# Routing the first two images as two groups of one in a conv-attention and mixture-of-experts kernel

## What is computed

```
x = x + conv_ref(ln_c(x))            # rmsnorm, qkv, softmax of q over dims, of k over pixels,
                                     # context = k v^T, out = context q, W_out, rmsnorm
t = to_tokens(x)                     # (16, 1024, 128)
logits = ln_t(t) @ gate_w + gate_b   # 8 experts
top2 of softmax(logits)
t = t + sum over both experts e of  p_e * (gelu(ln_t(t) @ W1[e] + b1[e]) @ W2[e] + b2[e])
```

## Time and profile before

| what | value |
|---|---|
| median of 3 runs | 974.99 us (972.36 to 977.9) |
| profiled execution | 973.93 us |
| its span, first to last instruction | 972.1 us |
| mean granted TensorE clock | 0.872 of full |
| PE busy | 699.5 us (72%) |
| POOL busy | 596.0 us (61%) |
| DVE busy | 589.4 us (61%) |
| ACT busy | 505.0 us (52%) |
| mean DMA rate | 178 GB/s |

### The profile page before, as it was taken

The page is one execution under the profiler, slowest core; times in us unless marked ns, Lnnn a source line. Parts: engine busy times, 40 slices in busy tenths (PEclk is TensorE's granted clock), DMA queues, the critical chain, the costliest instruction groups (busy, mean ns, idle before and its releaser), DMA issues. The chain is left out here.

```text
span 972.1 us, 15703 instructions
## 1 busy us (share of the span) xinstructions
PE 699.5 (72%) x4357; PEld 598.2 (62%) x4357; DVE 589.4 (61%) x1913; ACT 505.0 (52%) x980; POOL 596.0 (61%) x602
## 2 busy tenths in 40 slices
PE   4645738696979596969696878778796886778700
PEld 2433626686868485858585867666675775667600
DVE  2587484849475958495848676776768555233322
ACT  2423223675757566657656666756765544335400
POOL 1013636534457577757777677757775777777374
PEclk9867666897979898979998998989997998989955
DMA  6301012656656675766676776766566776779622
GB/s 165 104 22 36 30 57 75 212 171 199 188 185 199 191 224 165 228 206 192 205 221 190 226 219 198 207 211 207 170 212 201 221 238 205 254 234 309 221 77 63
DMA packets 120574, 173.46 MB, mean 178 GB/s; under 512 B 20504, under 2 KB 82600, under 8 KB 120488
## 3 DMA queue, kind: packets, MB, share of 16 engines
q1 hardware_dynamic: 103352, 138.65, 46.6%
q0 software_dynamic: 16384, 33.59, 11.5%
q10 hardware_dynamic: 752, 0.21, 0.1%
HBM read 112.86 MB, written 62.14 MB: 180 GB/s over the span
## 5 line engine op out<-in xcount | busy, mean ns | idle before, releaser
L465 POOL DMA_INDIRECT rows_in<-xf_tok,row_of x256 | 257.2, 1005 | 100.0 <-issue 77.6
L479 POOL DMA_INDIRECT y_rows<-rows_out,row_back x256 | 250.2, 977 | 93.3 <-issue 69.7
L1005 PE MATMUL y_ps<-wb,hid 128*128 128x128 f32 x1472 | 212.7, 291 | 65.8 <-DVE yb L869 56.0
L1005 PEld LDWEIGHTS y_ps<-wb,hid 128*128 128x128 f32 x1472 | 201.9, 205 | 90.1 <-issue 60.4
L559 ACT ACTIVATE hid<-h_ps,wb 128x256 f32<-128x256 f32 x368 | 158.4, 473 | 106.5 <-PE h_ps L995 104.8
L995 PE MATMUL h_ps<-xt,wb 128*128 128x256 f32 x736 | 204.3, 403 | 0.0
L869 DVE TENSOR_TENSOR yb<-y_ps,wb 128x256 f32<-128x256 f32 x184 | 77.4, 421 | 159.4 <-PE y_ps L1005 158.9
L995 PEld LDWEIGHTS h_ps<-xt,wb 128*128 128x128 f32 x736 | 137.3, 205 | 19.2
L553 ACT ACTIVATE xt<-t_ps 128x256 f32<-128x256 f32 x184 | 70.7, 384 | 131.2 <-PE t_ps L986 130.3
L919 PE MATMUL ab<-wqkv_t,x_sb 128*128 128x384 f32 x256 | 109.8, 524 | 10.2 <-ACT qkv L517 10.0
L517 ACT ACTIVATE qkv<-ab,r 128x384 f32<-128x384 f32 x128 | 73.3, 582 | 61.5 <-PE ab L919 36.2
(11 more groups left out here) (151 smaller groups left out, 1068.8 us busy)
## 6 DMA issues: line engine op xcount, KB each, us to landing
wb<-experts SPq DMA_DIRECT2D x184, 321.0 KB, 3.9
xb<-rows_in SPq DMA_DIRECT2D x184, 128.0 KB
rows_out<-yb SPq DMA_DIRECT2D x184, 128.0 KB
rows_in<-zeros SPq DMA_DIRECT2D x78, 128.0 KB, 2.2
x_sb<-in_x_dram SPq DMA_DIRECT2D x16, 512.0 KB, 4.0
out_dram<-out_sb SPq DMA_DIRECT2D x32, 256.0 KB, 3.5
rows_in<-xf_tok,row_of POOLq DMA_INDIRECT x256
y_rows<-rows_out,row_back POOLq DMA_INDIRECT x256, 2.9
```

The lines of the kernel that those rows point to most:

```text
L465: pool.indirect_dma_start(out=rows_in[group_of(n) % 2], out_offset=bass.IndirectOffsetOnAxis(ap=row_of[:, n % X1_RING, k, t:t + 1], axis=0 ...
L479: pool.indirect_dma_start(out=y_rows[:, r, k, :], out_offset=None, in_=rows_out[p % OUT_BUFS][0:BLOCKS[p] * ROWS, :], in_offset=bass.Indir ...
L1005: last = pe.matmul(y_ps[:, i * P:(i + 1) * P], hid[:, q % 2, k, i * P:(i + 1) * P], wb[:, r, HIDDEN + k * CH:HIDDEN + (k + 1) * CH], start ...
```

## The change

The first group of two images becomes two groups of one image each. All the rest of the code follows from that tuple.

```diff
-GROUPS = (2,) * 8
+GROUPS = (1, 1) + (2,) * 7
```

## The result

The changed kernel took 991.71 us (median, 989.68 to 993.48) and the kernel before, on the same chip, 975.25 us. The ratio is 1.0169, with a 95% interval of 1.0132 to 1.0205. So it is slower by 1.7%, clear of noise. The prediction was 990.0 with a range of 976 to 1003. The profiled execution took 990.69 us around a span of 988.9 us, 16.8 us more than before's.

A forecast was written before the change was run, and what follows sets the result against it. No engine bounds the whole: DVE sets nearly every stretch from r_rms to r2, PE or POOL the stretches between. Terms of +22.8 less 6.5 gave +16.3 us on 973.93, so 990 us, range 976 to 1003.

The forecast's parts named there:

- D0: Slots 82-94, end of r_rms to next r2: the added plan finds no idle DVE time, +3.8 us (at most 4.4).
- Q2: Slots 126-146, r2 to end of r_rms: nine blocks for one, set by PE, 25.69 to 32.0 us, +6.3.
- Q3: Slots 158-178, r2 to end of r_rms: denser blocks plus attention take PE 32.1 us, before 30.11, +2.0 (0 to +4.6).
- D1: Slots 114-126, end of r_rms to r2: first blocks start, one more bias add, plan 0.5 shorter, +1.3 us (+0.5 to +4).
- D2: Slots 146-158, end of r_rms to r2: blocks in flow, six bias adds for four, +3.1 us (+1.7 to +4).
- D4: Slots 210-222, end of r_rms to r2: blocks start again, with adds, some 19.2 for 18.29 us, +0.9 (0 to +1.9).
- Q4: Slots 190-210, r2 to end of r_rms: one block for seven, but POOL's queue with nine fetches sets 30.9 us, +3.4.
- D3: Slots 178-190, end of r_rms to r2: six pairs of adds on DVE, fewer bias adds, +2.0 us (-1.0 to +3.9).
- Q5, D5 and Q6: Slots 222-274, three stretches between r2 and r_rms: fetches moved earlier, relief of 0.7, 2.7 and 3.1 us, 6.5 together.
- It fits: Rival, chance 0.08: early blocks fit PE's idle time and fetches POOL's; 968 us, with Q2 and Q4 under 27 us.
- Paid back: Rival, chance 0.15: Q2 grows only to 27.46 us, D3 and Q4 shrink; 973 us, no difference.
- Starved: Rival, chance 0.08: with six buffers, loads of the 30 dense blocks wait for bias adds; +16 on the forecast, 1006 us.

The follow-up runs named there:

- another kernel: The kernel before, pairs kept, with seven more, empty blocks (30 for 23) in the first pair's same 64 slots: 984.6 us, ratio 1.0103.
- the changed kernel with late plans: The changed kernel with all nine plans moved from slot 88 to slot 103: 962.2 us, ratio 0.9878 to the kernel before.
- The kernel with late fetches: The changed kernel with fetches of images 0 and 1 back at slots 234 and 266, with one more buffer each for two tables: 985.8 us, ratio 1.0115.
- the kernel with image 0's plan late: The changed kernel with only image 0's plan moved from slot 88 to slot 103: 988.6 us, ratio 1.0148 to the kernel before.

## Why the prediction was right

**The plan.** Predicted +3.8, measured 3.91 on DVE and 3.92 in D0, and 3.91 us came back when it moved. The argument from DVE's full D0 held.

**Dense blocks.** The price of 2.0 us a block and 13.5 us for attention gave 31.5 for Q2. PE was busy 32.02 us. The same stretch came out to the hundredth in another kernel. Its count of some 205 matmuls for Q2 was too low, since 224 ran, but the time did not rest on it. Q3 was priced by the same sum at 32.1 and measured 34.19: it was undersized by 2.1 us. PE was busy 33.86 us in it for the 224 matmuls that took 32.02 in Q2, and two windows of it (PE's busy time alone, the clock, and the DMA share and rate) show where the clock was low:

```profile
201.00:204.00 3.00, 3.00 (x16) 0.62 0.84 251
204.00:207.00 3.00, 3.00 (x26) 1.00 0.83 225
```

In the changed kernel with late plans the clock in Q3 is 1.00, and the 224 matmuls take PE 32.29 us. So the term that I left out is the low clock at the start, 1.8 us. The present idle time of 2.3 us, by which my bound reached +4.6, did not stay: PE was idle for 0.3 us.

**D1 and D2.** D1 was +2.7 for +1.3. The bias add of the first block stood behind the plan on DVE, and PE waited 8.1 us for it with the single `y_ps`:

```profile
PE y_ps L1005 <- DVE yb L869: 8.1, 1, 8.1
```

So the matmul for the maxima behind it (L926) was late and DVE in turn waited 1.7 us. D2 was +1.0 for +3.1: I had taken D4 before, 18.29 us, as a D with blocks in flow, but in it a down product ran at half clock (2.0 us), and DVE was busy only 15.47 of the 18.29 us: my sentence that DVE is busy nearly all the time in every D did not hold for D4. In the changed kernel D2 passes at a clock of 1.00 and takes 17.06. Both terms were mis-sized, by +1.4 and -2.1, and the errors partly cancel.

**Fetches.** Q4 at +3.2 for +3.4 is the step most worth the work: the stretch that lost its blocks grew. The kernel with late fetches shows it the other way. D3 was 1.3 more than predicted. DVE is busy 22.16 us in D3, and 19.00 in the kernel without these adds: they cost 3.2 where I had 2.7 less 0.6 for bias adds. D4 went 1.4 us the other way; it is 18.19 us in the kernel with image 0's plan late, so a part of that is scatter. The relief in Q5, D5 and Q6 was 6.1 for 6.5.

**The rivals.** *It fits* asked for Q2 and Q4 under 27 us: they were 32.34 and 30.62. The higher early clock that spoke for it came (0.84 for 0.54 in D1, 1.00 for 0.61 in Q2), as the Trainium skill's rule has it (TensorE: Matmul & The Clock Gate, The HAM clock gate), and changed nothing in the sum, since Q2 is full at the higher clock. The prediction read the clocks before too smoothly as 1.00 where blocks are: D2, D3 and D4 have blocks too and stand at 0.79, 0.75 and 0.81. *Paid back* asked for a Q2 of 27.5 and a shrinking Q4. *Starved* did not come: in D1 PE waits 0.4 us for blocks' loads, and Q2 and Q3 have PE busy 99% of the time.

**Tables.** The changed kernel has 78 table loads for 76, 39 of them gelu's for 38. Seven stand in D1 and Q2, where there were none, and they are inside the measured stretches. The drain that the Trainium skill adds to each (ScalarE: Activation LUTs, What ACT_TABLE_LOAD costs) was not needed for any term, and no experiment separated it.

The sum hides errors of up to 2.1 us in single terms. That the shift came out at 16.8 for 16.3 is in part luck; that it was slower, and where, is not.

## What to carry over

Cut the trace at the points where engines hand over to each other, and ask of each stretch which engine is full in it. In this trace work on the full engine cost about its full length, and work on another cost little until that engine was full too. Here a plan costs 4.4 us in one half of a period and some 0.5 to 2 us in the other, and moving eight of them won some 21 us by the ratio, where the new grouping lost 16.5. When work leaves a stretch, look for the next queue: here fetches on POOL took all that the blocks had freed. And when an order is edited by hand, look at each wait for a buffer: one that costs nothing can come to cost much. The first store of a pair waited 9.4 us at no cost that shows; with the fetches three slots later it waited 15.4 us, the kernel lost 38 us, and 28 of them came back with a third buffer.

## What the runs showed of the hardware

Some stretches repeat to within 0.1 us between separate kernels with the same order: Q2 is 32.34, 32.34 and 32.33 us in three of them, D1 21.60, 21.64 and 21.61, and Q10 is 30.54 to 30.57 in seven. Others do not, though all seven have the same order there: Q7 is 31.15 to 32.32, Q11 30.71 to 31.65 and Q13 30.59 to 31.62. Whole runs of one kernel scatter by some 3 us to either side. So a single stretch in a profile can tell apart effects that the medians can't, but only after a look at how far that stretch scatters.

A fetch holds POOL for 0.95 us at the median and a send for 0.97, and 0.30 us of issue stand ahead of most of them. SP issues in order, so a store that waits holds back the loads behind it: here SP issued nothing for 15.4 us.
